# A mixture-of-experts block: the router's operands change sides, and the attention steps get new slots

## What is computed

```python
logits = x @ router_w.T                                   # (2048, 256) @ (256, 8)
probs = jax.nn.softmax(logits.astype(jnp.float32), axis=-1)
top_w, top_i = jax.lax.top_k(probs, TOP_K)                # TOP_K = 2
top_w = top_w / jnp.sum(top_w, axis=-1, keepdims=True)
...
shared_out = jax.nn.sigmoid(x @ shared_gate_w)[:, None] * shared
return (routed + shared_out).reshape(B, S, Hd)
```

## Time and profile before

| | us |
|---|---|
| median of 3 runs (604.96 to 609.38) | 605.73 |
| the profiled execution, whole | 608.32 |
| its span | 605.9 |
| TensorE busy | 526.0 (87%) |
| VectorE busy | 394.4 (65%) |
| ScalarE busy | 261.8 (43%) |
| GpSimd busy | 112.4 (19%) |
| mean granted TensorE clock | 0.931 of full |

### The profile page before, as it was taken

One profiled execution on the slowest core, in us unless ns is written; L12 is line 12 of the kernel. 1 busy time (PEld: TensorE's weight loads), 2 busy tenths in 40 slices (PEclk: granted clock), 3 DMA queues, 4 the chain that ended last, 5 costly groups with the idle time before them and its releaser, 6 DMA issues.

```text
span 605.9 us, 8087 instructions
## 1 busy us (share of the span) xinstructions
PE 526.0 (87%) x2464; PEld 416.9 (69%) x2464; DVE 394.4 (65%) x1159; ACT 261.8 (43%) x465; POOL 112.4 (19%) x133
## 2 busy tenths in 40 slices
PE   2835358999669999999999998999998999999981
PEld 1413234678555687886678786888886799999871
DVE  6786644788774798876488792332649566766437
ACT  4721444625365424365621525311243556666404
POOL 1510003200002323002205000031006024444400
PEclk9985679999769999999999999799998989999997
DMA  8981000000010002111001010010007224444274
GB/s 277 417 235 36 2 2 0 2 10 26 35 35 1 0 19 88 36 35 36 0 2 71 0 36 35 1 41 30 35 8 262 63 64 131 117 140 123 70 273 138
DMA packets 29548, 44.41 MB, mean 73 GB/s; under 512 B 3211, under 2 KB 24203, under 8 KB 29163
## 3 DMA queue, kind: packets, MB, share of 16 engines
q1 hardware_dynamic: 24515, 32.95, 16.9%
q0 software_dynamic: 3408, 9.38, 4.1%
q10 hardware_dynamic: 1584, 1.57, 0.9%
HBM read 27.55 MB, written 16.34 MB: 72 GB/s over the span
## 4 chain that ended last, share of the span: by engine, by line
PE 74%; DVE 16%; ACT 5%; DMA 3%; issue 2%; POOL 0%; ACTq 0%; POOLq 0%; DVEq 0%; SPq 0%
PE psum L768 15%; PE psum L727 12%; PE psum L728 12%; PE psum L729 12%; PE psum L794 5%; PE psum L843 3%; PE psum L737 3%; PE psum L815 3%; DVE XC L1223 2%; PE psum L811 2%; PE psum L829 2%; PE psum L918 1%; PE psum L935 1%; DMA QKV<-x 1%; PE psum L965 1%
## 5 line engine op out<-in xcount | busy, mean ns | idle before, releaser
L637 ACT ACTIVATE SM<-psum 128x512 f32<-128x512 f32 (+1 forms) x56 | 33.3, 596 | 135.0 <-PE psum L729 93.4
L1348 DVE TENSOR_TENSOR SM<-SM,psum 128x512 f32<-128x512 f32 (+1 forms) x56 | 38.3, 683 | 52.4 <-ACT SM L637 48.1
L513 POOL DMA_INDIRECT x_dispatched<-XN,dest x32 | 35.5, 1109 | 163.2 <-DVE XN L1416 154.6
L768 PE MATMUL psum<-WOU,SM 128*128 128x256 f32 x256 | 59.8, 379 | 0.0
L794 PE MATMUL psum<-WQKV,HT 128*128 128x512 f32 (+1 forms) x128 | 51.4, 554 | 6.3 <-ACT QKV L572 2.7
L504 POOL TENSOR_TENSOR OG<-QKV,hvec 128x256 f32<-128x256 f32 x16 | 13.4, 835 | 230.2 <-ACT IG L579 213.4
L768 PEld LDWEIGHTS psum<-WOU,SM 128*128 128x128 f32 x256 | 48.3, 189 | 10.1 <-issue 2.9
L522 POOL DMA_INDIRECT y_routed<-GO,g_dest x39 | 37.7, 967 | 64.1 <-ACT GO L702 63.4
L794 PEld LDWEIGHTS psum<-WQKV,HT 128*128 128x128 f32 x128 | 26.4, 214 | 29.7 <-issue 23.5
L768 PE MATMUL psum<-SDN,SM 128*128 128x256 f32 (+1 forms) x192 | 44.6, 381 | 0.0
L768 PEld LDWEIGHTS psum<-SDN,SM 128*128 128x128 f32 (+1 forms) x192 | 35.8, 189 | 6.6 <-issue 1.3
(11 more groups left out here) (292 smaller groups left out, 1321.2 us busy)
## 6 DMA issues: line engine op xcount, KB each, us to landing
XG<-x_dispatched SPq DMA_DIRECT2D x39, 130.0 KB, 2.7
YF<-y_routed SPq DMA_DIRECT2D x4, 1024.0 KB, 9.1
RUPR<-rup SPq DMA_DIRECT2D x1, 2816.0 KB
X<-x SPq DMA_DIRECT2D x4, 512.0 KB, 6.4
x_after_attention<-X SPq DMA_DIRECT2D x4, 512.0 KB, 2.8
QKV<-x ACTq DMA_DIRECT2D x3, 512.0 KB
y_shared<-SH SPq DMA_DIRECT2D x3, 512.0 KB, 2.9
SHF<-y_shared SPq DMA_DIRECT2D x1, 1536.0 KB
```

What stands on the lines that cost most here:

```text
L513: nc.gpsimd.indirect_dma_start(XD[:, :], bass.IndirectOffsetOnAxis(dest[:, i, old + j:old + j + 1], 0), XN[:, j, :], None).then_inc(dispat ...
L637: nc.scalar.activation(SM[0:rows, g % 3, 0:tb], p_pair(n)[0][0:rows, 0:tb], ACT.Silu).then_inc(silu_ready, 1)
L768: last = nc.tensor.matmul(p_down[:, j // 2, (j % 2) * D:(j % 2 + 1) * D], SM[0:rows, g % 3, j * P:(j + 1) * P], weight[0:rows, m, :], star ...
L1348: nc.vector.tensor_tensor(SM[0:rows, g % 3, 0:tb], SM[0:rows, g % 3, 0:tb], value_rows(n, rows)[:, 0:tb], ALU.mult).then_inc(hid_ready, 1)
```

## The change

1. The router's weights, padded to 128 columns, become the stationary operand, and 512 tokens are the moving operand: six matmuls of 512 columns for a block, and the logits come out with experts on partitions.
2. ScalarE copies nine rows of them to SBUF (LGT, which lies in SH; so it waits until SH of the block before has been stored). A new step, logit, transposes LGT back in four pieces on TensorE; VectorE then copies to LG as before. In blocks 0 to 2 logit directly follows route in `ORDER`; in block 3 one shared down step (sdn 3) lies between.
3. The wider router weights need room: wr, wg16, wmean and wgx now lie under RUPR and RDNR. So SP issues the load of RUPR only once they have been used (`wr_lo`, `wg_ready`), and the load of RDNR, under wgx, only after the last mup of block 3, behind the third store of SH.
4. The slots of attention steps in `PLACE` are new for all four engines; the first attention list too has a row of its own there (zeros for PE, ACT and DVE). Of TensorE's steps, beside the MLP of block 0: og goes ahead of mdn 7. Beside that of block 1: mup 0 ahead of q 0, mdn 0 ahead of q 2. Beside that of block 2: mup 2 ahead of g 1, mdn 3 ahead of mt, og from behind hid 0 to behind hid 2, wo from behind hid 2 to behind sdn 1, and xt ahead of h2. On ScalarE, beside the MLP of block 0, g 1 goes ahead of mup 1's SiLU; on VectorE in block 0 norm 1 goes ahead of mup 6, and o ahead of sum 0.

```diff
-RP = RW + 1
+RP = P
...
-            order += [("xt", b, 0), ("route", b, 0), ("choose", b, 0)]
-    route = {4: [("xt", b, 0)], 5: [("route", b, 0), ("choose", b, 0)], 6: [("choose", b, 1)], 7: [("choose", b, 2)],
+            order += [("xt", b, 0), ("route", b, 0), ("logit", b, 0), ("choose", b, 0)]
+    route = {4: [("xt", b, 0)], 5: [("route", b, 0)], 6: [("logit", b, 0), ("choose", b, 0), ("choose", b, 1)], 7: [("choose", b, 2)],
              8: [("rank", b, 0), ("choose", b, 3)]}
...
+            wr, wg16, wmean, _, wgx = (first_names.enter_context(nc.sbuf_tensor(k, s, F32)) for k, s in (
+                ("wr", [P, C, RP]), ("wg16", [P, C, HEADS]), ("wmean", [P, C, HEADS]),
+                ("under_rupr", [P, E * C * GU - C * (RP + 2 * HEADS)]), ("wgx", [P, C, D])))
...
+        LGT = SH[:, :, :].rearrange("p j d -> p (j d)")[0:RW, 0:TB]
...
             sp.dma_start(SDN[:, :, :], sdn).then_inc(w_in["sdn"], 16)
+            sp.wait_ge(wr_lo, 1)
+            sp.wait_ge(wg_ready, 1)
             sp.dma_start(RUPR[:, :, :, :], rup).then_inc(w_in["routed"], 16)
-            sp.dma_start(RDNR[:, :, :, :], rdn).then_inc(w_in["routed"], 16)
...
             sp.wait_ge(up_psum, done("mup", NB - 1, FM - 1))
+            sp.dma_start(RDNR[:, :, :, :], rdn).then_inc(w_in["routed"], 16)
             sp.wait_ge(x2_kept, 16 * NB)
...
+                if stage == "route":
+                    act.wait_ge(rt_psum, b + 1)
+                    if b > 0:
+                        act.wait_ge(sh_kept, 16 * b if b < NB - 1 else 16 * (b - 1))
+                    nc.scalar.activation(LGT[:, 0:tb], p_token(b)[0:RW, 0, 0:tb], ACT.Copy).then_inc(rt_kept, 1)
...
                     part_h, part_l = token_parts(b)
+                    for c in range(C):
+                        last = mm3(p_token(b)[:, 0, 0:tb], wrH[:, c, :], wrL[:, c, :], part_h[:, c, 0:tb], part_l[:, c, 0:tb],
+                                   c == 0, c == C - 1)
+                    last.then_inc(rt_psum, 1)
+                if stage == "logit":
+                    pe.wait_ge(rt_kept, b + 1)
                     for j in range(nj):
-                        t = slice(j * P, (j + 1) * P)
-                        for c in range(C):
-                            last = mm3(p_token(b)[:, 0, j * RP:(j + 1) * RP], part_h[:, c, t], part_l[:, c, t], wrH[:, c, :], wrL[:, c, :],
-                                       c == 0, c == C - 1)
-                    last.then_inc(rt_psum, 1)
+                        last = nc.tensor.transpose(p_token(b)[:, 1, j * RW:(j + 1) * RW], LGT[:, j * P:(j + 1) * P], ident[0:RW, 0:RW])
+                    last.then_inc(rt_turned, 1)
...
-                if stage == "route":
-                    dve.wait_ge(rt_psum, b + 1)
-                    nc.vector.tensor_copy(LG[:, 0:nj, :], p_token(b)[:, 0, 0:nj * RP].rearrange("p (j r) -> p j r", r=RP)[:, :, 0:RW]).then_inc(rt_copied, 1)
+                if stage == "logit":
+                    dve.wait_ge(rt_turned, b + 1)
+                    nc.vector.tensor_copy(LG[:, 0:nj, :], p_token(b)[:, 1, 0:nj * RW].rearrange("p (j r) -> p j r", r=RW)).then_inc(rt_copied, 1)
```

More of the change, by code:

```diff
@@ L154, in steps @@
 def steps(engine):
-    attention = [(PLACE[engine][b][i] if b >= 0 else 0, s[0], b + (s in AHEAD), s[1]) for b in range(-1, NB)
+    attention = [(PLACE[engine][b + 1][i], s[0], b + (s in AHEAD), s[1]) for b in range(-1, NB)
                  for i, s in enumerate(ATTENTION) if 0 <= b + (s in AHEAD) < NB]
@@ L225, in build @@
         with ExitStack() as first_names:
+            wr, wg16, wmean, _, wgx = (first_names.enter_context(nc.sbuf_tensor(k, s, F32)) for k, s in (
+                ("wr", [P, C, RP]), ("wg16", [P, C, HEADS]), ("wmean", [P, C, HEADS]),
+                ("under_rupr", [P, E * C * GU - C * (RP + 2 * HEADS)]), ("wgx", [P, C, D])))
+        with ExitStack() as first_names:
             RUPR = first_names.enter_context(nc.sbuf_tensor("RUPR", [P, E, C, GU], F32))
@@ L237, in build @@
         hvec = sb("hvec", [P, 4, HD])
-        wr, wrH, wrL = sb("wr", [P, C, RP]), sb("wrH", [P, C, RP], F32R), sb("wrL", [P, C, RP], F32R)
-        wg16, wgx = sb("wg16", [P, C, HEADS]), sb("wgx", [P, C, D])
-        wmean = sb("wmean", [P, C, HEADS])
+        wrH, wrL = sb("wrH", [P, C, RP], F32R), sb("wrL", [P, C, RP], F32R)
         st, mv = sb("st", [P, J, 6]), sb("mv", [P, J, 2])
@@ L307, in build @@
         up_psum, silu_ready, hid_ready, hid_used, mlp_read = map(sem, ("up_psum", "silu_ready", "hid_ready", "hid_used", "mlp_read"))
-        x2_stats, xn_ready, xt_psum, xt_hi, xt_lo, rt_psum, rt_copied = map(
-            sem, ("x2_stats", "xn_ready", "xt_psum", "xt_hi", "xt_lo", "rt_psum", "rt_copied"))
+        x2_stats, xn_ready, xt_psum, xt_hi, xt_lo, rt_psum, rt_turned, rt_kept, rt_copied = map(
+            sem, ("x2_stats", "xn_ready", "xt_psum", "xt_hi", "xt_lo", "rt_psum", "rt_turned", "rt_kept", "rt_copied"))
         lmax_ready, exp_ready, picked, rank_psum, shared_gate = map(
```

## The result

The changed kernel takes 603.8 us (median of 17 runs, 600.4 to 606.6), beside 606.0 for the kernel before on the same chip; the ratio is 0.9935, 95% interval 0.9914 to 0.9956. The ratio compares the means (603.2 and 607.2); on 605.7 it is 3.9 us less (2.7 to 5.2), where 5.05 were forecast. The two medians are only 2.2 us apart. One thing must be known to read these numbers: the 81 runs of the kernel before fall into two groups, 44 at 603.5 to 607.0 and 37 at 608.3 to 610.3 (mean granted clock 0.934 and 0.925, where it was noted), so its median wanders between 605.8 and 608.9 from one comparison to the next, and I compare the medians of the variants with one another and give the ratio for each.

The account below looks back on a forecast made before the run. TensorE, busy 526 of 605.9 us, was taken as the bound, falling short in three turns between token blocks. Terms 2.0 + 1.4 + 1.0 + 0.85 - 0.2 = 5.05 us, or 0.83%, gave 600.7 us; range 596.5 to 605.5.

Parts of the forecast that it names:

- Block 0, 2.0: Turn after block 0: earlier gate product and Wo, x2n at 167.6, mup from 179.35 instead of 181.35; gain 2.0 us.
- Block 1, 1.4: Turn after block 1: router chain loses 0.3 us, q behind it wins back 1.67 at full clock; gain 1.4 us.
- Block 2, 1.0: Turn after block 2: mup from 381.85 instead of 382.85, its slow first six stay; gain 1.0 us, between 0.4 and 3.0.
- Rival (a): Clock holds everywhere, block 0 back at full clock 1.3 us sooner, block 2 gaining 3.0; 597.4 us, chance 0.17.
- Block 3, 0.85: Block 3's router: a down step hides the logit copy, rank matmuls and table chain come 0.85 us sooner.
- Start, -0.2: Kernel start: wr grows to 256 columns, VectorE's product is on the chain; loss 0.2 us, between 0 and 0.3.
- the other moves, 0: Remaining attention steps at new slots, under a full TensorE: worth nothing; the tightest, in block 2, has 0.9 us of cover.
- RDNR, 0: RDNR load issued near 452.4, landing by 460.0 before ScalarE needs it near 460.2; loss 0, at most 3.1 us.
- The estimate from the Trainium skill's 341 GB/s: RDNR with its store takes near 8.4 us, landing at 460.9; loss 0.7 us, time 601.4.
- (b): Standstill at the logit step costs clock: block 1's q or mup stays slow, block 2's gain goes; 603.1 us, chance 0.17.
- (c): Placement without effect, block 0's turn bound by something missed, block 2's slack gone; 604 to 606 us, chance 0.08.
- (d): RDNR shares engines evenly, lands near 472, ScalarE and TensorE wait; 612.5 us, chance 0.05, plus 0.03 for 606 to 610.

Follow-up runs that it names:

- e9: Changed kernel with RDNR loaded earlier, the logit step behind mup 0 and useless matmuls in block 0's waits; 597.7 us, ratio 0.9840.
- e3: Changed kernel with the RDNR load issued earlier, in front of SP's wait for the last x_after store; 601.7 us, ratio 0.9912.
- e1: Changed kernel with the attention steps at the places of the kernel before; 605.8 us, ratio 0.9989.
- e4: Changed kernel with the RDNR load issued behind the x_after and y_shared loads in SP's queue; 616.3 us, ratio 1.0149.
- e6: Changed kernel with the attention steps at their old places and the RDNR load issued earlier; 602.6 us, ratio 0.9921.
- e11: Changed kernel with the RDNR load issued earlier and useless matmuls in block 0's waits, logit step not moved; 598.0 us, ratio 0.9860.
- e12: Changed kernel, late RDNR load kept, with useless matmuls in block 0's waits; 601.1 us, ratio 0.9904.

## Why the prediction was right, and where it was wrong

The class (no change beyond 1%) and the range held, with 603.8 in 596.5 to 605.5. The forecast of 5.05 us less was 1.1 too much by the ratio and 2.9 by the medians, and its terms erred in both directions: 0.9 too much in block 0, 2.2 too little in block 2, 2.1 to 3.3 left out for RDNR and 2.6 for the end. That the sum came near is in part luck.

**Block 0, 2.0.** Measured 1.1. VectorE's chain came as reckoned: Wo at 155.33, and x2n at 167.66 for 167.6. The step that failed is "ScalarE first finishes the HT copies (168.6), so XN, XTH and HN shift 1.4 us". The clock fell at 163.3, in the 7.18 us wait behind Wo; the eight transposes for HT took 1.97 us and not 1.09, and XN followed at 169.64, 0.3 before the old 169.93:

```profile
168.30 1.45 ACT L578 ACTIVATE HT<-psum,vec 128x512 f32<-128x512 f32 x2 [7.36 <-PE psum L755]
169.64 2.07 ACT L658 ACTIVATE XN<-X,x2n,x2r 128x256 f32<-128x256 f32 x4
```

With the clock held, in e9, XN starts 0.87 us sooner, counted from the down step at 150.30 (151.06 in e9). So mup 0 started at 180.03 for 179.35, and 0.7 of the missing 0.9 stands there. The rest is behind it: I let the old 1.5 us of slow clock stand behind the logit step, and the clock returned only at 183.8, eight matmuls into mup, which cost 1.8. In e3, the same program up to there, it returned at 180.2, and from the same down step on (150.30, and 151.24 in e3) e3 gained 1.9 more. Of 8.7 us of busy time lost in this turn before, the changed kernel loses 6.5, its siblings with the wide router 3.6 to 7.1.

**Block 1, 1.4.** Measured 1.6, with q at full clock. But the cause that I gave, that the clock falls behind narrow matmuls and wide ones keep it, holds at most as a chance: it fell there in one of four profiles. Part of the gain was luck of the profile that I started from the earlier trace rows.

**Block 2, 1.0.** Measured 3.2 in the profile, above my upper end of 3.0. It is counted from the 2.6 at the transposes of XN. The failed step is "1.3 slow as the clock fell after six matmuls before" and the slow first six of mup that were to stay: with six wide matmuls the clock stayed at 1.00. Rival (a) had this right for this block. e1 shows the part of the places here: without them 1.44 us go to the wait for H2L, a wait that the prediction did not price when it said that the transposes for h2 fill the wait for XTL.

**Block 3, 0.85.** Measured 0.6; then the clock fell from 446.6 to 450 behind the rank matmuls and took 1.7 us of it.

**Start, -0.2, and the other moves, 0.** The lead was 0.4 at 93 us and -0.1 at 150. In block 2 the cover of 0.9 us held: the shout copies follow the last down step as before. I had called the forecast wrong if TensorE idled more than 1 us between 195 and 365, and it idled 1.66. That mark was badly set: 0.90 is the q wait that was priced, moved across the edge from 194.8 to 198.0, and 0.76 the standstill of block 1, priced too.

**RDNR, 0.** This is the step that failed. The medians put it at 2.1, 3.0 and 3.3 us (three pairs) where I took the lower bound of 0; the upper was 3.1. Three errors met. The bound of 4.7 us took the best rate on the page of the profile, 417 GB/s, for a tile of 88 partitions; alone in e3 the load moves at 144 GB/s and takes 10.1 us. Its landing at 460.47 was just what I forecast, 460.0, but only because it was issued at 447.2 and not at 452.4. And "free until about 460.2" was counted from a split at 459.04 less 0.85, though the terms of blocks 0 to 2 add 4.4 us of lead ahead of it; with the 6.3 us that were there ScalarE was ready at 454.35, and VectorE, which was through with the table chain at 459.5, stood for its result until 461.95. The marks set for this load were a first split by 460.2 and a wait for hid 3.3 of at most 2.4; they read 460.47 and 2.04, so they hardly showed a loss of 2 us. The estimate from the Trainium skill's 341 GB/s named the right sign (by its own terms the store and the load take 8.7 us and not 8.4), and as a rate it was more than twice too fast for this shape. The Trainium skill's rule on going round between queue rows did not come to bear: the loads compared stand in one queue, SP's, and e4 shows their order.

**The end, not in the sum.** The lead of 5.4 us at the first group shrank to 2.8. 0.8 went between the issue of the last y_routed store and that of the YF load behind it (565.92 to 569.18, before 571.24 to 573.74), and 1.7 to the clock from 576 to 580 in the final sum, as the table by stage shows. The profiles of e1 and e3 have no low clock in the final sum, those of e6 to e9 lose about as much.

**Rivals.** (b), slow q behind block 1's standstill, did not come. (c) is excluded by Wo at 155.33. (d), a late load, came in kind, but smaller than even its small part (606 to 610) and not by an even share of the engines; e4 reached its price of 612.5 and more. (a) was right for block 2.

The best version found is e9, 597.7 us and 0.984 (0.9802 to 0.9877) of before; e11, without the later logit step, is as fast within what was measured.

## What to carry to other kernels

Before a load is moved late, date its first use in the kernel after, not in the one before, and take its speed from its own shape; and let no wait cover two loads of which one is early. Where a turn between stages leaves TensorE idle, the low clock that follows costs as well, and matmuls without use in the gap may pay (here 1.6 to 4.9 us). A step that is wide on one engine lengthens the chain of handovers, so what stands behind it in the order of another engine must be moved ahead in the same change.

## What the runs showed of the hardware

- TensorE's granted clock is a matter of chance at the same place of the same program: block 2's turn at 1.00 in the changed kernel and at 0.93 in e3, block 0's back at 183.8 and at 180.2. The Trainium skill, page "TensorE: Matmul & The Clock Gate", section "Part 1: The HAM clock gate (the "warmup" mystery)", calls the number of slow matmuls at a kernel's start run-variable; these runs show the same far behind the start.
- A load of 88 partitions x 16 KB moved at 144 GB/s alone, on 0.66 of the DMA engines (e3).
- Useless matmuls in three waits (28, 7 and 6) kept the clock at 1.00 through 42 us that had 0.76 to 0.80 without them (e9 and e11; 0.96 in e12, where it fell at 179.4 behind a wait of 1.79 us for the logit copy).
- The four transposes of the 9 x 512 logits take 0.34 us at full clock (284.63 to 284.97), less than the 0.45 of the lower bound that was taken from the router's narrow matmuls.
